# A decoder block on one core: state products behind the second own terms, second scores behind the first state products, key roots inverted by halves

## The chip, the core and the metric

One core of one Trainium2 chip runs the whole kernel. The metric is the device time in microseconds (us). PE is the matmul engine, PEld its weight loads, DVE, ACT and POOL the vector, scalar and general engines, SP the engine that issues most DMAs. Each engine runs its own list of instructions in program order; they meet only at semaphores.

## The reference

Three blocks follow each other on x of shape (16, 64, 256), each with a residual and a layernorm: a test-time-training recurrence, a cross attention over a context of 64 tokens, and a feed-forward block with int8-like rounding. The change touches the first block's loop and the scale of the attention keys. The recurrence goes over 4 chunks of 16 tokens, for each batch b and each of 16 heads of width 16:

```
kh      = k_i @ S                          # "state product" with the keys
g       = w * norm(kh) + b - (v_i - k_i);  v_new = norm-backward(g * w)
A       = tril(q_i @ k_i^T) * eta          # "scores"
qh      = q_i @ S - A @ v_new              # state product and "own term"
o       = q_i + (w * norm(qh) + b)
S       = S - (k_i * eta)^T @ v_new        # the own terms' other half
```

In the cross attention the scores are divided by the root mean square of each key over its 128 features (rmsnorm of k), head by head.

## The kernel before, in words

**Layout of the recurrence.** 16 batches and 16 heads are laid out as 32 groups g of 4 partition strips j. Each of the three products is 128 matmuls of 32x32 weights, for one half h (0 or 1) of the groups: `state_products(c, h)` (L508, recorded at L518), `own_terms(c, h)` (L522, recorded at L528) and `scores_ttt(c, h)` (L493, recorded at L500). Every matmul has a weight load of its own. State products read the state `st`, start the accumulation of `q S`, `k S` and S itself in PSUM; own terms add the new rows `ub` times the masked scores `ak`.

**The loop for chunk c and half h.** PE's `state_products(c, h)` ends; DVE's `state_read(c, h)` (L1425) copies kh, squares and sums it; ACT's `state_root` takes the root; DVE's `chain(c, h)` (L1432, 12 operations, then four `ub` writes, L1462) makes the update; PE's `own_terms(c, h)` adds it; DVE's `after_own_terms(c, h)` (L1511) copies qh and the new state, which releases `state_products(c + 1, h)`. DVE's own order within a chunk is: `state_read(c, 0)`; `kb_rows`, `a_masked`, `output_inverse(2c - 2)`, `out_c(c - 2)` (in chunk 1 the first two stand ahead of the read, the last two are absent); `chain(c, 0)`; `state_read(c, 1)`; `output_sums(2c - 1)`; `output_inverse(2c - 1)`, which waits for ACT's `output_root(2c - 1)` (L1080); `chain(c, 1)`; `out_normed`; `after_own_terms(c, 0)`; `out_gated(c - 1)`; `after_own_terms(c, 1)`; `output_sums(2c)`.

**The keys as filler.** Between these products PE makes the keys of the cross attention: 32 units (`key_unit`, PE L652, ACT L1065). A unit is one product into bank 6 or 7 (L659, two instructions), then on ACT a square (L1071) and a scaled copy (L1073). PE sums the squares of units four at a time (L650, eight instructions; units 0 to 3 right behind the matmul of unit 4, units 4 to 7 behind that of unit 8, and so on). A unit's square on ACT waits, from unit 4 on, for the sum of the unit four before it; a unit's matmul waits for the copy of the unit two before it. How many units stand at each place is in `KEY_PLACES`, read by the PE list and, with places merged, by the ACT list; ACT has its roots and squares of the recurrence between them.

**After the loop.** ACT takes the roots of all key sums (`krow`, L1076). PE runs `warm(4, 8)`, eight matmuls that nobody reads, waits for `k_rooted`, and begins a pipeline over 8 tiles of 128 tokens: `ttt_out` (L834), transposes (L842), `q_quarter` (L724), scores of the attention (L767), and so on. SP writes the key roots to DRAM and reads them back with other rows in two halves (`kroot`, `kinv`), DVE inverts both halves in one reciprocal (`key_scales`, L1549), and SP writes `kscale` and loads it, broadcast, as `rkb` for each tile. DVE's `scores_out(0)` (L1707) multiplies the first tile's scores by `rkb`; ACT's `exp_p(0)` depends on it and stands on ACT ahead of tile 1's second quarter. In that pipeline's step 0, DVE does `last_scale`, `last_gate`, `last_square`, `last_scale`, `last_out(2)`, which releases `ttt_out(2)` on PE, and then `key_scales`.

Of the kernel before, what the change touches and what calls it, by code (L numbers as in the profile page):

```python
# [36 lines left out]
B, T, D = 16, 64, 256  # L37
# [17 lines left out]
LT = NT - 1  # L55
KEY_PLACES = [(1, 2), (2, 2, 1, 1, 2, 1), (2, 2, 1, 1, 2, 1), (2, 3, 3, 3)]

def decoder_block(nc, x, ctx_in, Wq, Wk, Wv, Wo, Wbeta, ln_w, ln_b, Wg1, Wg2, norm_w,  # L60
                  XWq, XWk, XWv, XWo, gq, gk, w1_in, w2_in, out):
    stack = ExitStack()
    with stack:
# [315 lines left out]
        def _(sp):  # L379
# [36 lines left out]
            def roots_to_rows(half):  # L416
                sp.wait_ge(sem("k_rooted"), 1)
                for odd in range(2):
                    at = 64 * half + 32 * odd
                    sp.dma_start(kroot[half].rearrange("b (r o) t -> o r b t", o=2)[odd],  # L420
                                 krow[at:at + XH // 2, :].rearrange("p (b t) -> p b t", t=T)).then_inc(sem("k_rows_out"), 16)
                sp.wait_ge(sem("k_rows_out"), 32 * (half + 1))
                sp.dma_start(kinv[:, half * T:(half + 1) * T], kroot[half].rearrange("b h t -> (b h) t")).then_inc(sem("k_roots_in"), 16)

            def scales_out(half):
                sp.wait_ge(sem("k_inverted"), 1)
                sp.dma_start(kscale[half * B // 2:(half + 1) * B // 2, :].rearrange("b (h t) -> (b h) t", t=T),
                             kinv[:, half * T:(half + 1) * T]).then_inc(sem("k_scales_out"), 16)
# [43 lines left out]
        def _(pe):  # L472
# [204 lines left out]
            for c in range(1, NCH):  # L677
                places = iter(KEY_PLACES[c])
                state_products(c, 0)
                keys(next(places))  # L680
                state_products(c, 1)
                keys(next(places))
                if c < NCH - 1:
                    scores_ttt(c + 1, 0)
                    keys(next(places))
                own_terms(c, 0)
                if c < NCH - 1:
                    keys(next(places))
                    scores_ttt(c + 1, 1)
                keys(next(places))  # L690
                own_terms(c, 1)
                for n in places:
                    keys(n)
            key_unit(next(units))
# [149 lines left out]

            warm(4, 8)
            pe.wait_ge(sem("o_feat"), NCH)
# [104 lines left out]
        def _(act):  # L951
# [159 lines left out]
            for c in range(1, NCH):  # L1111
# [4 lines left out]
                output_square(c - 1)  # L1116
                keys(places[0])
                if c < NCH - 1:
                    k_blocks(c + 1)
                keys(places[1])  # L1120
                output_root(2 * c - 1)
                state_root(c, 1)
                for n in places[2:-2]:
                    keys(n)
                keys(places[-2])
                gated_square(c - 1)
                if c < NCH - 1:
                    keys(places[-1])
            last_root(0)
# [175 lines left out]
        def _(dve):  # L1305
# [240 lines left out]

            def key_scales():
                dve.wait_ge(sem("k_roots_in"), 32)
                V.reciprocal(kinv[:, :], kinv[:, :]).then_inc(sem("k_inverted"), 1)  # L1549

# [10 lines left out]
            for c in range(1, NCH):  # L1561
# [4 lines left out]
                if c >= 2:  # L1566
                    kb_rows(c)
                    a_masked(c)
                    output_inverse(2 * c - 2)
                    out_c(c - 2)  # L1570
                chain(c, 0)
                state_read(c, 1)
# [174 lines left out]
            for i, cur, prev, last2, last3, nxt, nxt2 in pipeline():  # L1747
                if i == 0:
                    last_scale(qhR, 2)
                    last_gate(2)  # L1750
                    last_square(sup, 3)
                    last_scale(sup, 3)
                    last_out(2)
                    key_scales()
                if nxt2:
# [195 lines left out]
```

## Time and profile before

| | |
|---|---|
| median of 3 runs | 381.57 us (378.9, 381.57, 383.26) |
| the profiled execution | 382.47 us, of which the span 380.7 us |
| PE, PEld busy | 344.8 us (91%), 242.8 us (64%) |
| DVE, ACT, POOL busy | 264.5 us (69%), 201.3 us (53%), 75.6 us (20%) |
| mean granted TensorE clock | 0.974 of full speed |
| chunks 1 to 3 of the recurrence | from about 70 to 146 us of the span |

The span counts from the first to the last instruction; the time has the launch around it. A clock of 1.0 is 2.4 GHz, 0.5 is 1.2 GHz. "Issue" in a row is idle time in which an engine waited for nothing that the profile shows. In a timeline, consecutive instructions of one line are merged, and a new row begins where there was a pause.

### The profile page before, as it was taken

To read this page: it belongs to the slowest core of one execution; us is meant where nothing else is said; L and a number is where in the kernel's file an instruction comes from. 1 tells how busy PE (TensorE), PEld (TensorE's weight loads), DVE (VectorE), ACT (ScalarE), POOL (GpSimd) and SP (SyncE) were. 2 spreads that over 40 slices of the span, in tenths; PEclk is the share of its full clock that TensorE was granted. 3 is DMA by queue.
4 is the path that set the end of the run, shared out by engine and by line. 5 is a ranking of instruction groups with operands and counts; after the bars stand their busy time and mean duration, and the time that the engine had idled before them with its cause. 6 is when DMAs were issued, how large, how long until landed. Compare 5 with 4: busy or idle time off the path is not lost.

```text
span 380.7 us, 11631 instructions
## 1 busy us (share of the span) xinstructions
PE 344.8 (91%) x5095; PEld 242.8 (64%) x5098; DVE 264.5 (69%) x536; ACT 201.3 (53%) x371; POOL 75.6 (20%) x91
## 2 busy tenths in 40 slices
PE   1999997998979877998999999999999999999974
PEld 1544585455435332587698796896977969866731
DVE  0499997897797899556263674855846739566795
ACT  1245974855525635255516556555555566576351
POOL 3009300000000000000062341522714505300100
PEclk9999999999987968999999999999999999999998
DMA  8997000000402001029120100200201000000000
GB/s 195 277 289 248 4 4 3 5 3 23 151 4 83 34 2 58 16 53 203 31 57 0 50 8 15 58 0 16 57 1 56 16 15 0 2 15 0 16 1 28
DMA packets 17986, 19.96 MB, mean 52 GB/s; under 512 B 3712, under 2 KB 15376, under 8 KB 17680
## 3 DMA queue, kind: packets, MB, share of 16 engines
q1 hardware_dynamic: 17328, 18.69, 18.8%
q8 instruction: 40, 0.66, 0.8%
q10 hardware_dynamic: 608, 0.54, 0.7%
q14 instruction: 10, 0.08, 0.1%
HBM read 18.04 MB, written 1.18 MB: 50 GB/s over the span
## 4 chain that ended last, share of the span: by engine, by line
PE 73%; DVE 15%; ACT 4%; issue 3%; DMA 3%; SPq 0%; POOLq 0%; POOL 0%; DVEq 0%
PE ps L790 14%; PE ps L724 12%; PE ps L547 6%; PE ps L659 5%; PE ps L782 5%; PE ps L767 4%; PE ps L500 3%; PE ps L809 2%; PE ps L528 2%; PE ps L740 2%; PE ps L518 2%; PE ps L617 2%; PE ps L650 2%; PE ps L758 2%; DMA xn<-in_x_dram 2%
## 5 line engine op out<-in xcount | busy, mean ns | idle before, releaser
L724 PEld LDWEIGHTS ps<-x1t,xwq 128*128 128x128 f32 x512 | 59.2, 192 | 6.4 <-issue 4.2
L724 PE MATMUL ps<-x1t,xwq 128*128 128x128 f32 x512 | 62.1, 278 | 0.7 <-ACT x1t L1188 0.7
L790 PE MATMUL ps<-mvo,cxp 128*128 128x256 f32 x224 | 51.8, 383 | 0.5 <-ACT cxp L1199 0.5
L1893 POOL TENSOR_SCALAR rstd<-mv 128x1 f32<-128x1 f32 x20 | 4.4, 218 | 212.6 <-DVE mv L1635 212.6
L790 PEld LDWEIGHTS ps<-mvo,cxp 128*128 128x128 f32 x224 | 41.3, 190 | 6.6 <-ACT cxp L1199 0.8
L659 PE MATMUL ps<-ctxt,xwk 128*128 128x512 f32 x64 | 39.1, 727 | 3.5 <-ACT kt L1073 2.3
L1151 ACT ACTIVATE qt<-ps 128x512 f32<-128x512 f32 x32 | 19.1, 596 | 33.9 <-PE ps L724 33.9
L1071 ACT ACTIVATE ksq<-ps 128x512 f32<-128x512 f32 x32 | 18.9, 591 | 21.4 <-PE ps L659 13.4
L1073 ACT ACTIVATE kt<-ps,gks 128x512 f32<-128x512 f32 x32 | 21.9, 683 | 0.0
L1158 ACT ACTIVATE qsq<-ps 128x512 f32<-128x512 f32 x32 | 19.0, 593 | 4.2 <-PE ps L740 4.2
L659 PEld LDWEIGHTS ps<-ctxt,xwk 128*128 128x128 f32 x64 | 11.9, 217 | 14.3 <-ACT kt L1073 6.2
L528 PEld LDWEIGHTS ps<-ak,ub 32*32 32x32 f32 x1024 | 11.9, 109 | 13.7 <-issue 13.5
L767 PEld LDWEIGHTS ps<-kt,qt 128*64 128x64 f32 x512 | 16.2, 138 | 6.8 <-ACT qt L1151 3.8
L528 PE MATMUL ps<-ak,ub 32*32 32x48 f32 (+1 forms) x1024 | 13.4, 200 | 6.9 <-DVE ub L1462 3.5
L1644 DVE TENSOR_SCALAR x<-rr,mv,rstd 128x256 f32<-128x256 f32 x16 | 6.6, 412 | 18.7 <-POOL rstd L1894 18.5
L782 PE MATMUL ps<-pt,ctx 64*128 64x512 f32 x64 | 18.5, 638 | 0.7 <-ACT pt L1178 0.7
L767 PE MATMUL ps<-kt,qt 128*64 128x64 f32 x512 | 18.4, 225 | 0.0
L1707 DVE TENSOR_TENSOR pr<-ps,rkb 128x1024 f32<-128x1024 f32 x8 | 9.8, 1224 | 12.2 <-PE ps L767 8.7
L1199 ACT ACTIVATE cxp<-ps 128x512 f32<-128x512 f32 x28 | 15.3, 606 | 4.5 <-PE ps L782 4.5
L1683 DVE TENSOR_TENSOR gs<-ps,s 128x352 f32<-128x352 f32 x16 | 8.3, 522 | 13.4 <-PE ps L809 13.2
L1908 POOL TENSOR_TENSOR rq<-rq,mhalf 128x16 f32<-128x16 f32 x6 | 17.4, 2908 | 0.5
L500 PEld LDWEIGHTS ps<-kqi,kb 32*32 32x32 f32 x1024 | 10.1, 110 | 7.8 <-issue 6.8
(238 smaller groups left out, 683.2 us busy)
## 6 DMA issues: line engine op xcount, KB each, us to landing
rkb<-kscale SPq DMA_DIRECT2D x16, 256.0 KB, 4.2
ctx<-in_ctx_dram SPq DMA_DIRECT2D x4, 512.0 KB, 8.7
xwo<-in_L_xattn_Wo_dram SPq DMA_DIRECT2D x1, 2048.0 KB, 14.2
xwq<-in_L_xattn_Wq_dram SPq DMA_DIRECT2D x4, 512.0 KB, 4.8
w1n<-in_L_ffn_w_gate_up_dram SPq DMA_DIRECT2D x1, 1408.0 KB, 9.9
xwv<-in_L_xattn_Wv_dram SPq DMA_DIRECT2D x1, 1024.0 KB, 11.2
xwk<-in_L_xattn_Wk_dram SPq DMA_DIRECT2D x1, 1024.0 KB, 16.5
xn<-in_x_dram SPq DMA_DIRECT2D x2, 512.0 KB, 5.9
```

The source lines that it names most:

```text
L500: last = mm(ps[part, 4 * BANK + g * C:4 * BANK + (g + 1) * C], kb[part, g * 32:(g + 1) * 32], kq[part, col:col + C], start=True, stop=True)
L528: last = mm(ps[part, g * GW + C:g * GW + C + w], ub[part, g * 32:(g + 1) * 32], ak[part, g * (C + 32):g * (C + 32) + w], start=c == 0 and ...
L547: last = mm(bank(bk), w[:, k * D + hh * P:k * D + (hh + 1) * P], xt[:, k * B * T + half * BANK:k * B * T + (half + 1) * BANK], start=k == ...
L659: mm(bank(6 + n % 2), xwk[:, h * XD:(h + 1) * XD], ctxt[:, half * BANK:(half + 1) * BANK], start=True, stop=True)\
L724: last = mm(bank(n % 2, P, t * P), xwq[qn][:, k * BANK + t * P:k * BANK + (t + 1) * P], x1t[:, (i % 2) * D + k * P:(i % 2) * D + (k + 1) * ...
L767: last = mm(ps[b2 * T:(b2 + 1) * T, 4 * BANK + h * T:4 * BANK + (h + 1) * T], qt[:, h * P + b2 * T:h * P + (b2 + 1) * T], kt[:, (i * XH + ...
L782: turn_done(mm(bank(bk), ctx2[rows, b * CD:(b + 1) * CD], pt[rows, :].rearrange("p (h q) -> p h q", q=P)[:, :, b2 * T:(b2 + 1) * T], start ...
L790: last = mm(bank(turn_banks[turn_of[("y", i, 0)]], D), context_of(i)[:, h * P:(h + 1) * P], mvo[:, h * D:(h + 1) * D], start=h == 0, stop= ...
L1071: A(ksq[n % 4][:, :], bank(6 + n % 2), ACT.Square).then_inc(sem("k_squared"), 1)
L1073: A(o, bank(6 + n % 2).rearrange("p (i t) -> p i t", t=P), ACT.Copy, scale=gks[:, 1:2]).then_inc(sem("key_emptied"), 1)
L1151: A(qt[:, qn * BANK:(qn + 1) * BANK], bank(n % 2), ACT.Copy).then_inc(sem("q_copied"), 1)
L1158: A(qsq[:, (n % 2) * BANK:(n % 2 + 1) * BANK], bank(n % 2), ACT.Square).then_inc(sem("q_squared"), 1)
```

## The change

It reorders three lists and cuts one instruction in two; except for five dummy matmuls nothing is added to or taken from the arithmetic.

- PE, loop: `scores_ttt(2, 1)` and `(3, 1)` move from between the own terms of the chunk before to behind the first state products of their own chunk. Behind `own_terms(c, 1)` no key units are left, so that the next chunk's state products follow directly.
- The key units' places are new. Per chunk, with s for state products, o for own terms, a for scores and numbers for units: before, chunk 1 was s0 2 s1 2 a(2,0) 1 o0 1 a(2,1) 2 o1 1, and so was chunk 2; chunk 3 was s0 2 s1 3 o0 3 o1 3. After, chunk 1 is s0 3 s1 2 a(2,0) 1 o0 3 o1; chunk 2 is s0 1 a(2,1) 1 s1 2 a(3,0) 1 o0 4 o1; chunk 3 is s0 1 a(3,1) 2 s1 2 o0 3 o1, and 3 units after it.
- ACT, loop: ahead of `output_root(2c - 1)` and `state_root(c, 1)` stood 2 + 2 units in chunks 1 and 2; now 3 + 3 stand there in chunk 1 and 2 + 3 in chunk 2.
- DVE, loop: `a_masked(c)` goes behind `output_inverse` and `out_c`.
- `warm(4, 8)` becomes `warm(4, 3)`.
- `key_scales` is done by halves: the first at the head of step 0, the second where it was. SP's `scales_out(half)` waits for its own half.

```diff
--- before.py
+++ after.py
@@ -53,7 +53,7 @@
 GW = 2 * C + 32
 NKU = 2 * XH
 LT = NT - 1
-KEY_PLACES = [(1, 2), (2, 2, 1, 1, 2, 1), (2, 2, 1, 1, 2, 1), (2, 3, 3, 3)]
+KEY_PLACES = [(1, 2), (1, 2, 2, 1, 3), (1, 1, 2, 1, 4), (1, 2, 2, 3, 3)]
 
 
 
@@ -420,10 +420,10 @@
                     sp.dma_start(kroot[half].rearrange("b (r o) t -> o r b t", o=2)[odd],
                                  krow[at:at + XH // 2, :].rearrange("p (b t) -> p b t", t=T)).then_inc(sem("k_rows_out"), 16)
                 sp.wait_ge(sem("k_rows_out"), 32 * (half + 1))
-                sp.dma_start(kinv[:, half * T:(half + 1) * T], kroot[half].rearrange("b h t -> (b h) t")).then_inc(sem("k_roots_in"), 16)
+                sp.dma_start(kinv[:, half * T:(half + 1) * T], kroot[half].rearrange("b h t -> (b h) t")).then_inc(sem("k_roots_in%d" % half), 16)
 
             def scales_out(half):
-                sp.wait_ge(sem("k_inverted"), 1)
+                sp.wait_ge(sem("k_inverted"), half + 1)
                 sp.dma_start(kscale[half * B // 2:(half + 1) * B // 2, :].rearrange("b (h t) -> (b h) t", t=T),
                              kinv[:, half * T:(half + 1) * T]).then_inc(sem("k_scales_out"), 16)
 
@@ -678,19 +678,18 @@
                 places = iter(KEY_PLACES[c])
                 state_products(c, 0)
                 keys(next(places))
+                if c >= 2:
+                    scores_ttt(c, 1)
+                keys(next(places))
                 state_products(c, 1)
                 keys(next(places))
                 if c < NCH - 1:
                     scores_ttt(c + 1, 0)
                     keys(next(places))
                 own_terms(c, 0)
-                if c < NCH - 1:
-                    keys(next(places))
-                    scores_ttt(c + 1, 1)
                 keys(next(places))
                 own_terms(c, 1)
-                for n in places:
-                    keys(n)
+            keys(next(places))
             key_unit(next(units))
 
 
@@ -842,7 +841,7 @@
                     last = nc.tensor.transpose(bank(bk, P, k * P), xn[:, i * D + k * P:i * D + (k + 1) * P], ident[:, :])
                 last.then_inc(sem("tp_done"), 1)
 
-            warm(4, 8)
+            warm(4, 3)
             pe.wait_ge(sem("o_feat"), NCH)
             pe.wait_ge(sem("wo_scaled"), KT)
             pe.wait_ge(sem("key_emptied"), NKU)
@@ -1114,18 +1113,16 @@
                 if c >= 2:
                     output_root(2 * c - 2)
                 output_square(c - 1)
-                keys(places[0])
+                keys(places[0] + places[1])
                 if c < NCH - 1:
                     k_blocks(c + 1)
-                keys(places[1])
+                    keys(places[2] + places[3])
+                else:
+                    keys(places[2])
                 output_root(2 * c - 1)
                 state_root(c, 1)
-                for n in places[2:-2]:
-                    keys(n)
-                keys(places[-2])
+                keys(places[4] if c < NCH - 1 else places[3])
                 gated_square(c - 1)
-                if c < NCH - 1:
-                    keys(places[-1])
             last_root(0)
             output_root(2 * NCH - 2)
             keys(1)
@@ -1544,9 +1541,10 @@
                 o = ogt[:, :].rearrange("p (a b c s) -> p c a b s", a=KT, b=B, c=NCH)[:, c]
                 V.transpose(o, oR[:, :]).then_inc(sem("o_feat"), 1)
 
-            def key_scales():
-                dve.wait_ge(sem("k_roots_in"), 32)
-                V.reciprocal(kinv[:, :], kinv[:, :]).then_inc(sem("k_inverted"), 1)
+            def key_scales(half):
+                own = kinv[:, half * T:(half + 1) * T]
+                dve.wait_ge(sem("k_roots_in%d" % half), 16)
+                V.reciprocal(own, own).then_inc(sem("k_inverted"), 1)
 
             kb_rows(0)
             weights_rounded("w2")
@@ -1565,9 +1563,9 @@
                 state_read(c, 0)
                 if c >= 2:
                     kb_rows(c)
-                    a_masked(c)
                     output_inverse(2 * c - 2)
                     out_c(c - 2)
+                    a_masked(c)
                 chain(c, 0)
                 state_read(c, 1)
                 output_sums(2 * c - 1)
@@ -1746,12 +1744,13 @@
             dve.wait_ge(sem("ld_x"), 32)
             for i, cur, prev, last2, last3, nxt, nxt2 in pipeline():
                 if i == 0:
+                    key_scales(0)
                     last_scale(qhR, 2)
                     last_gate(2)
                     last_square(sup, 3)
                     last_scale(sup, 3)
                     last_out(2)
-                    key_scales()
+                    key_scales(1)
                 if nxt2:
                     bk = turn("wo", i + 2)
                     freed(V.tensor_tensor(rw[:, :], bank(bk, D), xn[:, (i + 2) * D:(i + 3) * D], ALU.add), "wo", i + 2)
```

## Rows read from the trace of the kernel before

**Rows 1.** Waits between 66 and 156 us; columns: engine, line, releaser, total us, times, longest

```profile
DVE khR L1427 <- PE ps L518: 4.3, 2, 2.2
...
DVE qhR L1513 <- PE ps L528: 2.8, 2, 1.7
```

**Rows 2.** Timeline of PE, chunk 1 into 2; columns: start us, us, instructions, [idle before]

```profile
81.92 1.94 PE L528 MATMUL ps<-ak,ub 32*32 32x48 f32 x128
...
85.77 1.06 PE L650 MATMUL ps<-ksq,onehot 128*32 128x512 f32 x8 [0.84 <-issue]
86.76 1.19 PE L500 MATMUL ps<-kqi,kb 32*32 32x16 f32 x120
89.22 0.25 PE L500 MATMUL ps<-kqi,kb 32*32 32x16 f32 x8 [1.26 <-issue]
...
91.31 1.82 PE L528 MATMUL ps<-ak,ub 32*32 32x48 f32 x128
...
94.12 1.80 PE L518 MATMUL ps<-kqi,st 32*32 32x64 f32 x113
96.77 0.42 PE L518 MATMUL ps<-kqi,st 32*32 32x64 f32 x15 [0.85 <-issue]
```

**Rows 3.** Timeline of PE, chunks 2 and 3

```profile
105.97 0.44 PE L500 MATMUL ps<-kqi,kb 32*32 32x16 f32 x31 [0.63 <-issue]
...
111.34 0.71 PE L528 MATMUL ps<-ak,ub 32*32 32x48 f32 x42 [1.82 <-issue]
...
135.52 1.80 PE L528 MATMUL ps<-ak,ub 32*32 32x16 f32 x128 [3.04 <-DVE ub L1462]
```

**Rows 4.** Timeline of DVE, chunks 1 to 3

```profile
82.08 0.35 DVE L1525 RECIPROCAL ors<-osd 128x32 f32<-128x32 f32 x1 [0.39 <-ACT osd L1080]
...
87.96 0.48 DVE L1462 TENSOR_SCALAR ub<-us__111,mask_h 128x128 f32<-128x128 f32 x2
...
97.25 0.45 DVE L1427 STREAM_TRANSPOSE khR<-ps 128x256 f32<-128x256 f32 x1 [2.23 <-PE ps L518]
...
101.36 0.71 DVE L1545 STREAM_TRANSPOSE ogt<-oR 128x512 f32<-128x512 f32 x1
...
110.18 0.35 DVE L1525 RECIPROCAL ors<-osd 128x32 f32<-128x32 f32 x1 [0.39 <-ACT osd L1080]
...
124.70 0.45 DVE L1427 STREAM_TRANSPOSE khR<-ps 128x256 f32<-128x256 f32 x1 [2.10 <-PE ps L518]
```

**Rows 5.** Timeline of ACT, chunk 1

```profile
81.72 0.32 ACT L1080 ACTIVATE osd<-ovs,eps_t 128x32 f32<-128x32 f32 x1 [0.56 <-DVE ovs L1521]
...
86.91 0.60 ACT L1071 ACTIVATE ksq<-ps 128x512 f32<-128x512 f32 x1 [3.61 <-PE ps L650]
```

**Rows 6.** Windows; columns: stretch, length, busy PE, PEld, DVE, ACT, POOL, granted clock, DMA

```profile
135.00:138.00 3.00, 2.48 (x129) 2.22 (x130) 2.52 (x7) 0.52 (x2) 0.00 (x0) 0.62 0.03 5
```

**Rows 7.** Timeline of PE after the recurrence

```profile
153.75 1.67 PE L643 MATMUL ps<-w1t,ident_b 128*128 128x512 bf16 x7 [0.16 <-issue]
155.26 1.89 PE L834 MATMUL ps<-wo,ogt 128*128 128x256 f32 x8
...
180.49 0.43 PE L740 MATMUL ps<-qsq,onehot 128*32 128x128 f32 x8 [0.98 <-ACT qsq L1158]
```

**Rows 8.** Timeline of ACT, the key roots

```profile
153.62 0.69 ACT L1076 ACTIVATE krow<-ps,eps_t 128x512 f32<-128x512 f32 x1 [0.77 <-PE ps L650]
```

**Rows 9.** Timeline of SP's queue, the first reload of key roots

```profile
156.32 0.35 SPq L423 DMA_DIRECT2D kinv<-kroot  x1
```

**Rows 10.** View of DMAs; columns: transfer, queue, count, KB each, median us to landing

```profile
kinv<-kroot SPq DMA_DIRECT2D x2, 32.0 KB, 2.5
```

**Rows 11.** Timeline of DVE, key inversion and first scores

```profile
165.69 0.91 DVE L1549 RECIPROCAL kinv<-kinv 128x128 f32<-128x128 f32 x1
...
173.15 1.23 DVE L1707 TENSOR_TENSOR pr<-ps,rkb 128x1024 f32<-128x1024 f32 x1 [3.56 <-DMA rkb<-kscale]
```

**Rows 12.** Chain of waits, in order of time; columns: start us, us, what

```profile
168.69 4.34 DMA rkb<-kscale
```

## The prediction

> **What bounds the kernel now.** The shares of busy time come first: PE has 91% of the span, so it looks like the bound everywhere. Inside the recurrence that is not so simple, and the waits between 66 and 156 us say how: twice DVE waits for the state products (L518), 4.3 us in all, and twice for the second own terms (L528), 2.8 us [rows 1]. Those 7.1 us are the boundaries between chunks 1 and 2 and between 2 and 3. The timeline of PE shows what PE did meanwhile: the rows of chunk 1 have the last `ub` of half 1 written at 87.96 + 0.48 = 88.44 us [rows 4], but the own terms that use it start at 91.31 [rows 2], because scores (2, 1) and two key units stand ahead. Behind them one unit precedes the state products, which end at 97.19, and DVE reads them at 97.25 [rows 2, 4]. The change takes both obstacles away. Read by this alone it gives the whole 7.1 us.
>
> Two other things in the same rows speak against that, and the sum rests on them.
>
> First, PE stops inside runs of small matmuls, waiting for nothing the profile shows. The halts stand at fixed counts: between 85.77 and 89.22 lie 8 + 120 = 128 matmuls; from 89.22 to 96.77 lie 8 + 4 + 128 + 2 + 113 = 255 [rows 2]. So there is a crossing every 128 matmuls, each with its weight load, whatever their size. From one crossing to the next PE never got quicker than 89.22 - 85.77 = 3.45 us where it halted; the crossing ahead of 96.77 lies 116 matmuls into the own terms, at 91.31 + 116/128 x 1.75 = 92.9, so that one took 3.9, and in chunk 2 one halt took 1.82 us at 111.34 [rows 2, 3]. The next stretch of instructions seems to arrive no earlier. A product of 128 small matmuls lasts 1.3 to 2 us, so key units between products cost PE nothing: they fill time in which it would halt. The change puts own terms, state products, one unit and scores in a row.
>
> The Trainium skill, "Runtime: NRT & Kernel Launch", section "Instruction fetch mechanics", says that instructions come in 16 KiB blocks of 256 and that crossing a block is "mostly hidden". The trace agrees with the 256, which are 128 matmuls with their loads, and not with the rest. By that rule the sum would be that of the first rival below.
>
> Second, the order on ACT. DVE's `output_inverse(1)` stands ahead of `chain(1, 1)` and waits for ACT's `output_root(1)`: 0.39 us at 82.08 [rows 4]. The root now stands behind unit 8 on ACT, and unit 8's square waits for a PE sum.
>
> **Part by part, recurrence.** Chunk 1, the root. Up to the first own terms PE does the same set of work in another order, so unit 8 starts where they did, 81.92 [rows 2]. A unit takes 0.92 us (two between 89.47 and 91.31), a sum group 0.99 (85.77 to 86.76) [rows 2]. The group starts at 82.85, and ACT gets unit 8 a further 86.91 - 85.77 = 1.14 us on [rows 2, 5], at 84.0. Square and copy take about 1.1 (two operations like the one of 0.60 [rows 5]), so the root starts at 85.1 instead of 81.72 [rows 5]; if the crossing that now falls ahead of the group halts PE by 0.3, at 85.4. `chain(1, 1)` shifts by 3.4 to 3.7, I take 3.5: `ub` is done at 88.44 + 3.5 = 91.95, and the own terms start at 92.0, 0.7 later than before rather than 2.8 earlier.
>
> Chunk 1 into 2. DVE was free for `khR` at 97.25 - 2.23 = 95.02, and without its earlier wait of 1.7 it would be free 95.02 - 1.7 - 88.44 = 4.9 us behind `ub` [rows 1, 4]: now at 96.85. PE: the crossing falls 114 matmuls into the own terms (eight more were done ahead of them), at 93.6, the next 114 into state products, no earlier than 93.6 + 3.45 to 3.9 = 97.05 to 97.5, though PE alone would be there at 95.5. With 14 matmuls left they end at 97.3 to 97.8. DVE reads at about 97.6, against 97.25: 0.4 later. The gain of the boundary is gone.
>
> Chunk 2. `a_masked(2)` behind `out_c` costs nothing: before, `out_c` ended 101.36 + 0.71 - 97.25 = 4.8 us after the read with `a_masked` ahead of it, an operation of the same 512 columns, so DVE gets to it after some 4.1 us [rows 4]; scores (2, 1) end 3.7 after the state products even with the next crossing. If that cover goes, its whole lateness is on the path. The root again stands behind a fourth unit, 16. From the end of the first state products (97.6) PE does units 12 to 16, one sum group, scores (2, 1) and (3, 0) and products (2, 1): 5 x 0.92 + 0.99 + 2 x 1.27 + 2.04 = 10.2 us (scores 120 in 1.19, products 113 in 1.80 [rows 2]). That is 107.8; three crossings at 3.65 each from 97.4 make it 109.6. ACT's root follows 1.14 + 1.1 later, DVE 0.36 after that: 110.4 to 112.2, against 110.18 [rows 4]. I take 112.2, 2.0 later, since these crossings follow with little between them. `ub` then is done 6.36 us after it (as 88.44 - 82.08), at 118.5. Four units and sums behind the own terms end by about 117 at full clock and are covered.
>
> Chunk 2 into 3. DVE is free at 118.5 + 4.9 = 123.4. Own terms start at 118.6; crossings fall 72 matmuls into them, 119.6, and 72 into the state products, not ahead of 119.6 + 3.45 to 3.9 = 123.1 to 123.5; the rest takes 0.6. DVE reads at about 124.0 to 124.4 rather than 124.70 [rows 4]: I take 0.3 earlier. Chunk 3 has the same DVE work, its own terms waited 3.04 us for `ub` [rows 3], and ACT's unit total ahead of the root is unchanged: nothing more moves. Sum: -0.3 us.
>
> **The clock.** PE idle for 3.04 us ahead of 135.52 was followed by 1.2 GHz: the granted share of 135 to 138 is 0.62 [rows 3, 6]. Now PE idles about 3 us ahead of 92.0, then has only small matmuls. If the clock falls there, units and sums in chunk 2 take twice as long, ahead of a root that is on the path. Between nothing and 3.4 us (half of the five units and one group that can stand in it, and what they push); I take 1.0, nearer to nothing since DVE covers some.
>
> **After the loop.** Five dummies of 1.67 / 7 = 0.24 us less, but PE needs the key roots, done at 153.62 + 0.69 = 154.31; `ttt_out` started at 155.26 [rows 7, 8]. Gain 0.9. At most 1.2, at least 0 if the clock falls for want of them.
>
> The key halves. The first `kinv` was sent at 156.32 and lands 2.5 later, 158.8 [rows 9, 10], ahead of step 0 (about 160.6, less 0.9), so DVE doesn't wait. It spends on it between 0.35 (128x32, [rows 4]) and 0.91 (128x128 [rows 11]), say 0.5, ahead of `last_out(2)`: counted whole on PE. In return `rkb` comes early: its load of 4.34 us [rows 12] ended the 3.56 us that DVE waited for the first scores [rows 11]; what ends last then is the scores themselves, 0.9 earlier. That reaches PE through `exp_p(0)` and the 0.98 us wait at 180.49 [rows 7]. Net gain 0.9 - 0.5 = 0.4; bounds +0.5 and -0.9. If `rkb` were still late, the 0.5 would stay.
>
> **Sum.** -0.3 + 1.0 - 0.9 - 0.4 = -0.6 us. The profiled execution took 382.47, 0.9 above the median of 381.57; off the median this is **381.0 us**.
>
> **Rivals.**
> - *Halts do not follow the order* (0.27). The next stretch arrives while PE waits for `ub`, so that products follow directly. Then DVE is the bound: it reads at 96.85 (-0.4); the root of chunk 2 comes at 109.8, also -0.4; `ub` at 116.15, DVE free at 121.05 against 124.70: -3.65, with -0.9 and -0.4 about -5: 376.6. For it: other stretches pass without a halt. Against: halts stand in every product that follows another closely. The full 7.1 us would need the root on ACT to be early, which the list excludes.
> - *Longer halts and a low clock* (0.2), the slower side. From 105.97, where scores resumed, to 111.34 a stretch took 5.4 us [rows 3]. At 5.4 instead of 3.65 both boundaries lose 1.75 and chunk 2's root 1.5 more, +5; with the clock's full 3.4 in place of 1.0, +7.4 on -0.6: up to 388. It decides once stretches in chunk 2 take over 4.7 us, or `own_terms(2, 1)` waits for its four units; from there 385.5 to 388.
> - *The forecast* (0.53): the gain is eaten by ACT's root and by the halts.
>
> A measurement of this kernel can hardly tell 1% (3.8 us): its own three runs spread by 4.4. **Chances**: faster than 377.8 0.27, within 1% 0.53, slower 0.20. The forecast alone has 378.5 to 384.5; to leave out no more than 2 in 10 I go from **376.3 to 386.0**.
>
> **What would show it.** `ors` (L1525) of chunk 1 waits some 3.5 us for `osd`, behind `kt` of unit 8: the first step. `own_terms(1, 1)` at about 92.0 and a halt inside the state products right behind: the second; no halt there, and DVE without a wait for L518, would be the first rival. The granted clock between 92 and 105 tells the clock's term. `scores_out(0)` should end its wait on PE, not on `rkb`. If `ors` is not late, my reading of ACT's list is wrong, and the time is near 374.

## The result, and the profile after

The changed kernel takes 386.62 us (median of 4 runs, 385.84 to 387.25), the kernel before, beside it and with its first runs, 380.31 us (4 runs). The ratio is 1.0155, 95% interval 1.0082 to 1.0228: slower by 1.6%, or some 6 us. The forecast of 381.0 and the range up to 386.0 are missed; the time lies where the rival "longer halts and a low clock" had it (385.5 to 388), though it got there only in part by that rival's path. An execution that is over 1.5% slower than the fastest of its kernel is left out of every ratio below.

The span of the profiled execution is 384.1 us against 380.7. Its head, ahead of the recurrence, happened to be 1.3 us shorter, so I count from one event of the recurrence, DVE's first `khR` of chunk 1 (72.13 before, 70.84 after). First DVE in the kernel after, where each bracket is idle time and what ended it (L1424 is `state_read`, L1522 `output_inverse`, L1510 `after_own_terms`, L1411 `a_masked`):

```profile
70.84 0.43 DVE L1424 STREAM_TRANSPOSE khR<-ps 128x256 f32<-128x256 f32 x1
...
84.25 0.35 DVE L1522 RECIPROCAL ors<-osd 128x32 f32<-128x32 f32 x1 [3.85 <-ACT osd L1079]
...
94.79 0.45 DVE L1510 STREAM_TRANSPOSE qhR<-ps 128x256 f32<-128x256 f32 x1 [1.06 <-PE ps L528]
...
98.28 0.45 DVE L1424 STREAM_TRANSPOSE khR<-ps 128x256 f32<-128x256 f32 x1 [1.72 <-PE ps L518]
...
104.23 0.69 DVE L1411 TENSOR_TENSOR ak<-ps,tri 128x512 f32<-128x512 f32 x1 [1.73 <-PE ps L500]
...
114.76 0.35 DVE L1522 RECIPROCAL ors<-osd 128x32 f32<-128x32 f32 x1 [2.10 <-ACT osd L1079]
...
126.15 0.45 DVE L1424 STREAM_TRANSPOSE khR<-ps 128x256 f32<-128x256 f32 x1
...
132.96 0.69 DVE L1411 TENSOR_TENSOR ak<-ps,tri 128x512 f32<-128x512 f32 x1 [2.59 <-PE ps L500]
...
142.75 0.35 DVE L1522 RECIPROCAL ors<-osd 128x32 f32<-128x32 f32 x1 [1.36 <-ACT osd L1079]
```

Two of the waits at the same places in the kernel before (the others are in rows 1 and 4):

```profile
120.83 0.45 DVE L1513 STREAM_TRANSPOSE qhR<-ps 128x256 f32<-128x256 f32 x1 [1.16 <-PE ps L528]
...
137.63 0.35 DVE L1525 RECIPROCAL ors<-osd 128x32 f32<-128x32 f32 x1 [0.39 <-ACT osd L1080]
```

The loss can be read off as a sum, since DVE's own work hasn't changed. The two middle columns are the waits, and the running loss adds up what each wait after has more than the wait before.

| place | wait before | wait after | running loss |
|---|---|---|---|
| `ors`, chunk 1, for ACT's root [rows 4] | 0.39 | 3.85 | +3.5 |
| `qhR` and `khR`, chunk 1 into 2, for PE [rows 1] | 1.68 + 2.23 | 1.06 + 1.72 | +2.3 |
| `a_masked(2)`, for scores (2, 1) | 0 | 1.73 | +4.1 |
| `ors`, chunk 2 [rows 4] | 0.39 | 2.10 | +5.8 |
| `qhR` and `khR`, chunk 2 into 3 [rows 1] | 1.16 + 2.10 | 0 | +2.5 |
| `a_masked(3)`, for scores (3, 1) | 0 | 2.59 | +5.1 |
| `ors`, chunk 3 | 0.39 | 1.36 | +6.1 |

Counted by starts instead of waits, the last row is +6.4 (142.75 - 70.84 against 137.63 - 72.13). So the boundaries that the change is about were gained in part: 1.1 us from chunk 1 to 2, and from chunk 2 to 3 all 3.3 us. Five new or longer waits, 10.5 us in all, took more than twice that.

These are single executions. The changed loop repeats well: `khR` of chunk 3 comes 55.3 us behind that of chunk 1 here and in the experiment "Only the loop" below. The old loop does not: 52.6 us in the kernel before, 55.6 in the experiment "Only what stands behind the loop", whose loop is the same. There DVE waited longer for the state products:

```profile
127.10 0.45 DVE L1427 STREAM_TRANSPOSE khR<-ps 128x256 f32<-128x256 f32 x1 [3.57 <-PE ps L518]
```

The sum shows where this execution lost; how much the change costs is told by the ratios. On ACT the first of the five looks like this (L1070 is the square of unit 8, L1079 the root; the unit's copy stands between them):

```profile
82.83 0.60 ACT L1070 ACTIVATE ksq<-ps 128x512 f32<-128x512 f32 x1 [1.90 <-PE ps L650]
...
83.89 0.32 ACT L1079 ACTIVATE osd<-ovs,eps_t 128x32 f32<-128x32 f32 x1
```

The root stands behind unit 8, and its square waited 1.90 us for PE's sums. Now PE across the first boundary and in the two second scores (L528 own terms, L518 state products, L500 scores):

```profile
90.74 1.39 PE L528 MATMUL ps<-ak,ub 32*32 32x48 f32 x113 [1.78 <-DVE ub L1459]
94.12 0.46 PE L528 MATMUL ps<-ak,ub 32*32 32x48 f32 x12 [1.99 <-issue]
...
94.43 3.80 PE L518 MATMUL ps<-kqi,st 32*32 32x64 f32 x127
...
101.02 1.04 PE L500 MATMUL ps<-kqi,kb 32*32 32x16 f32 x103
103.78 0.38 PE L500 MATMUL ps<-kqi,kb 32*32 32x16 f32 x25 [1.72 <-issue]
...
125.40 0.70 PE L518 MATMUL ps<-kqi,st 32*32 32x32 f32 x58 [1.60 <-issue]
...
127.09 1.15 PE L500 MATMUL ps<-kqi,kb 32*32 32x16 f32 x68
131.87 1.04 PE L500 MATMUL ps<-kqi,kb 32*32 32x16 f32 x60 [3.64 <-issue]
```

The count of 128 holds: 12 + 1 + 3 + 127 matmuls, two of the unit, eight of sums and 103 of scores lie between the halt that ended at 94.12 and the one that ended at 103.78, 256 in all, one crossing having passed without a halt in the slow state products. From 125.40 to 131.87 it is 58 + 2 + 68 = 128. But that stretch lasted 6.5 us, where I had taken 3.65. SP's queue shows what ran beside both second scores, the loads of x and of the attention's Wq (two of the last three at once, the third behind the loop):

```profile
94.72 0.38 SPq L381 DMA_DIRECT2D xwq<-in_L_xattn_Wq_dram  x1
95.14 1.94 SPq L381 DMA_DIRECT2D xn<-in_x_dram  x2
124.27 26.65 SPq L381 DMA_DIRECT2D xwq<-in_L_xattn_Wq_dram  x3
```

They are sent when `own_terms(1, 1)` and `out_gated(1)` are done, which now is shortly ahead of the second scores. And the state products at 94.43 take 3.80 us, 30 ns a matmul instead of 16:

```profile
92.00:93.00 1.00, 0.14 (x15) 0.04 (x1) 1.00 (x2) 0.00 (x0) 0.00 (x0) 0.99 0.00 0
93.00:94.00 1.00, 0.00 (x0) 0.00 (x0) 0.70 (x2) 0.23 (x1) 0.00 (x0) 0.50 0.00 0
...
96.00:99.00 3.00, 3.00 (x80) 2.38 (x72) 1.24 (x3) 0.00 (x0) 0.00 (x0) 0.50 0.82 263
```

The granted clock (the number behind the five engines) is 0.50 there, 1.2 GHz. It fell at about 93.0, inside the halt that ended at 94.12; before that PE had stood idle for 1.78 us ahead of 90.74 and then done 1.39 us of small matmuls. It was low once more around the halt of 3.64 us (0.69 from 126 to 129, 0.50 from 129 to 135). Over the whole execution the clock is nearly what it was, 0.972 against 0.974, for the kernel before had its low stretches elsewhere (0.50 from 114 to 117).

### The profile page after: what moved, and what is told of

It reads as the page before. It is cut to its first block, busy times and chain, and to the rows that moved or that the text cites. A ratio compares the mean times of both kernels' runs of the same rounds, so it can differ in the third digit from the quotient of the medians.

```text
span 384.1 us, 11625 instructions
## 1 busy us (share of the span) xinstructions
PE 343.0 (89%) x5093; PEld 242.1 (63%) x5093; DVE 264.6 (69%) x537; ACT 201.5 (52%) x371; POOL 75.7 (20%) x91
## 4 chain that ended last, share of the span: by engine, by line
PE 73%; DVE 14%; ACT 6%; issue 4%; DMA 1%; SPq 0%; POOLq 0%; POOL 0%; DVEq 0%
PE ps L789 14%; PE ps L723 13%; PE ps L547 5%; PE ps L766 5%; PE ps L781 4%; PE ps L659 4%; PE ps L500 3%; PE ps L518 3%; PE ps L808 2%; PE ps L739 2%; PE ps L650 2%; PE ps L617 2%; PE ps L833 2%; PE ps L757 2%; DMA xn<-in_x_dram 1%
## 5 line engine op out<-in xcount | busy, mean ns | idle before, releaser
L659 PE MATMUL ps<-ctxt,xwk 128*128 128x512 f32 x64 | 37.4, 694 | 3.4 <-ACT kt L1072 2.2
L1070 ACT ACTIVATE ksq<-ps 128x512 f32<-128x512 f32 x32 | 19.0, 594 | 24.9 <-PE ps L659 15.6
L528 PEld LDWEIGHTS ps<-ak,ub 32*32 32x32 f32 x1024 | 11.4, 105 | 15.7 <-issue 15.7
L528 PE MATMUL ps<-ak,ub 32*32 32x48 f32 (+1 forms) x1024 | 12.9, 197 | 9.1 <-issue 4.6
L500 PEld LDWEIGHTS ps<-kqi,kb 32*32 32x32 f32 x1024 | 10.2, 110 | 10.7 <-issue 9.7
```

The lines of the kernel that those rows point to most:

```text
L500: last = mm(ps[part, 4 * BANK + g * C:4 * BANK + (g + 1) * C], kb[part, g * 32:(g + 1) * 32], kq[part, col:col + C], start=True, stop=True)
L528: last = mm(ps[part, g * GW + C:g * GW + C + w], ub[part, g * 32:(g + 1) * 32], ak[part, g * (C + 32):g * (C + 32) + w], start=c == 0 and ...
L659: mm(bank(6 + n % 2), xwk[:, h * XD:(h + 1) * XD], ctxt[:, half * BANK:(half + 1) * BANK], start=True, stop=True)\
L1070: A(ksq[n % 4][:, :], bank(6 + n % 2), ACT.Square).then_inc(sem("k_squared"), 1)
```

## Experiments

All ratios are against the kernel before, measured beside them, with 95% intervals. 1% is 3.8 us.

**Only what stands behind the loop.**

```diff
 # on the kernel before
-            warm(4, 8)
+            warm(4, 3)
 ...
+                    key_scales(0)            # ahead of last_scale(qhR, 2)
 ...
-                    key_scales()
+                    key_scales(1)
```

> The kernel before with the two edits behind the loop alone: three dummy matmuls instead of eight, key roots inverted by halves. Theory 'loop' (all of the loss comes from the reordered recurrence): same as before or slightly faster, 0 to -1.3 us, most likely -0.6, since between krow and ttt_out some 0.7 us go and the halves give nothing. Rival 'tail' (the lost dummies or the earlier reciprocal cost something later): slower than before by over 1 us.

Measured: 381.54 us, ratio 0.9966 (0.9923 to 1.0009). The tail does not cost; a gain isn't shown.

**Only the loop.** The reverse edit, on the changed kernel.

> The changed kernel with its two edits behind the loop undone, so that only the reordered recurrence is left. Theory 'loop': slower than before by 5.5 to 7 us. Rival 'tail': within 3 us of before.

Measured: 389.87 us, 1.0199 (1.0109 to 1.0290), some 7.6 us slower, a little more than expected. The whole loss is the reordered recurrence; the rival "tail" falls.

**Roots ahead of the units on ACT.**

```diff
 # on the changed kernel
-                    keys(places[2] + places[3])
-                else:
-                    keys(places[2])
+                    keys(places[2])
                 output_root(2 * c - 1)
                 state_root(c, 1)
-                keys(places[4] if c < NCH - 1 else places[3])
+                keys(places[3] + places[4] if c < NCH - 1 else places[2] + places[3])
```

> The changed kernel, but on ACT output_root(2c-1) and state_root(c, 1) stand ahead of units 8, 16 and 24 instead of behind them. Theory 'roots' (the waits of 3.85, 2.10 and 1.36 us of L1522 for osd are on the path): they shrink to some 0.4 and the kernel gains 3 to 6 us on the changed one, ending near the kernel before. Rival 'halts and clock' (PE is so late through its halts and the low clock that the root's lateness is covered): gain under 1.5 us.

Measured: 381.78 us, 0.9986 (0.9942 to 1.0029), 1.7% better than the changed kernel. DVE in this kernel (L1520 `output_inverse`, L1409 `a_masked`):

```profile
81.29 0.35 DVE L1520 RECIPROCAL ors<-osd 128x32 f32<-128x32 f32 x1 [0.79 <-ACT osd L1079]
...
101.28 0.69 DVE L1409 TENSOR_TENSOR ak<-ps,tri 128x512 f32<-128x512 f32 x1 [1.68 <-PE ps L500]
...
128.01 0.65 DVE L1409 TENSOR_TENSOR ak<-ps,tri 128x512 f32<-128x512 f32 x1
```

The waits for the root are 0.79, 0.39 and 0.39 us where they were 3.85, 2.10 and 1.36. PE kept its full clock up to 123 us. `a_masked(2)` still waits 1.68. The theory "roots" holds; the gain, some 6.4 us, is even a little above the 3 to 6 that were expected. But it is not the price of the waits for the root alone. With the roots early `out_gated(1)` is early too, the second set of loads starts at 119.63, and the halt in scores (3, 1) is 0.37 us instead of 3.64: `a_masked(3)`, at 128.01, waits for nothing. So this run also cures the low clock and a part of what the loads did.

**Loads behind the loop.**

```diff
 # on the changed kernel
-            sp.wait_ge(sem("mg_done"), 2 * 2)
-            load_xwq(0)
-            load_x()
             sp.wait_ge(sem("og_ready"), 2)
-            load_xwq(1)
-            load_xwq(2)
             sp.wait_ge(sem("mg_done"), 2 * NCH)
+            load_x()
+            load_xwq(0)
+            load_xwq(1)
+            load_xwq(2)
             load_xwq(3)
```

> The changed kernel with the loads of x and of Wq of the attention (3 MB) all sent behind the last own terms instead of within chunks 2 and 3. Theory 'loads' (they hold up the instructions of PE: halts of 1.72 and 3.64 us in the second scores come while they run or just after): these halts fall below 1 us, the waits of L1411 (1.73 and 2.59 us) with them, and the kernel gains 2 to 5 us, less what the pipeline waits for its first data. Rival 'fixed' (a stretch of 128 matmuls takes its time whatever the loads do): halts as before, no gain or a loss of up to 2 us.

Measured: 382.19 us, 1.0028 (0.9987 to 1.0069), 1.3% better than the changed kernel with no compute instruction moved. The second scores of chunk 3 on PE, then DVE (L1410 `a_masked`):

```profile
128.41 0.69 PE L499 MATMUL ps<-kqi,kb 32*32 32x16 f32 x60 [1.01 <-issue]
```

```profile
103.62 0.65 DVE L1410 TENSOR_TENSOR ak<-ps,tri 128x512 f32<-128x512 f32 x1
...
129.85 0.65 DVE L1410 TENSOR_TENSOR ak<-ps,tri 128x512 f32<-128x512 f32 x1
```

The halt in scores (3, 1) is 1.01 instead of 3.64 us, in scores (2, 1) there is none, and `a_masked` waits for neither. "Fixed" falls: a stretch of instructions takes longer while the loads run. The price comes behind the loop, where DVE waits 1.72 us for the first `kinv`, whose DMA now meets the loads.

**Both, with the loads one step earlier.** The roots as above, and the loads of x and three parts of Wq sent after `own_terms(3, 0)`, where PE has key units and one last product.

```diff
 # on the kernel with the roots ahead
-            sp.wait_ge(sem("mg_done"), 2 * 2)
-            load_xwq(0)
-            load_x()
             sp.wait_ge(sem("og_ready"), 2)
+            sp.wait_ge(sem("mg_done"), 2 * NCH - 1)
+            load_xwq(0)
+            load_x()
             load_xwq(1)
```

> The changed kernel with the roots ahead of units 8, 16 and 24 on ACT, and with x and the first three parts of Wq loaded only once own_terms(3, 0) are done, so that no load runs beside the second scores. Theory 'two causes' (late roots and loads that hold up PE's instructions add up): some 3 us better than the roots alone, 376 to 380 us, and faster than the kernel before by 3 to 6 us; no wait of L1411, none of L1522 above 0.4. Rival 'one cause' (whichever is cured, the other's time comes back as a halt or a wait): no better than the roots alone, 380 to 383.

Measured: 378.5 us, 0.9923 (0.9898 to 0.9948), about 2.9 us faster than the kernel before. That is 0.6% better than the roots alone, with intervals that just overlap, and 2.3% better than the changed kernel, where roots and loads by themselves gave 1.7% and 1.3%. So curing both is better than curing one, but the two overlap and do not add up in full. The expected wait of at most 0.4 us for the root was missed in chunk 1, where it is 0.79. PE's halts and DVE's waits that remain:

```profile
93.01 0.33 PE L528 MATMUL ps<-ak,ub 32*32 32x48 f32 x12 [1.29 <-issue]
...
96.74 0.42 PE L518 MATMUL ps<-kqi,st 32*32 32x64 f32 x15 [1.80 <-issue]
...
122.30 0.70 PE L518 MATMUL ps<-kqi,st 32*32 32x32 f32 x58 [2.04 <-issue]
...
126.30 0.69 PE L500 MATMUL ps<-kqi,kb 32*32 32x16 f32 x60 [1.55 <-issue]
```

```profile
93.51 0.45 DVE L1508 STREAM_TRANSPOSE qhR<-ps 128x256 f32<-128x256 f32 x1 [2.26 <-PE ps L528]
...
97.22 0.45 DVE L1422 STREAM_TRANSPOSE khR<-ps 128x256 f32<-128x256 f32 x1 [1.94 <-PE ps L518]
...
123.04 0.45 DVE L1422 STREAM_TRANSPOSE khR<-ps 128x256 f32<-128x256 f32 x1 [1.51 <-PE ps L518]
```

No load runs here, the clock is full up to 126, and the halts are still there: 93.01 to 96.74 and 122.30 to 126.30 are stretches of 3.7 and 4.0 us. This is the floor that the prediction meant. DVE waits 2.26 + 1.94 us for it at the first boundary, about what it waited before the change (3.9), and 1.51 at the second, where it had waited 3.3. Neither `a_masked` waits. The pauses of 1.29 and 1.80 us at the place where the changed kernel lost its clock left it at 1.00 here.

**Dummy matmuls against the falling clock.**

```diff
 # on the changed kernel, between own_terms(c, 0) and own_terms(c, 1)
                 keys(next(places))
+                if c == 1:
+                    pe.wait_ge(sem("key_emptied"), 11)
+                    warm(6, 7)
                 own_terms(c, 1)
```

> The changed kernel with seven dummy matmuls (1.6 us) in PE's idle time ahead of own_terms(1, 1). Theory 'clock' (the idle ahead of it lets the clock fall, and the 127 state products at half clock, 3.80 us instead of 2, make khR of chunk 2 late): the clock stays at 2.4 GHz through 93 to 100, but a halt of about 1.5 us returns inside these state products, as the stretch of instructions is then the limit; gain 0 to 2 us. Rival 'clock is all': khR of chunk 2 comes 1.9 us earlier, the kernel gains 2 to 3 us.

Measured: 386.8 us, 1.0116 (1.0047 to 1.0184). The interval overlaps with that of the changed kernel, so the time alone decides nothing; the trace shows the place itself:

```profile
93.00:96.00 3.00, 2.06 (x136) 1.76 (x125) 2.90 (x6) 0.63 (x1) 0.00 (x0) 1.00 0.52 142
```

```profile
91.70 1.56 PE L528 MATMUL ps<-ak,ub 32*32 32x48 f32 x128 [0.42 <-DVE ub L1462]
...
95.95 0.53 PE L518 MATMUL ps<-kqi,st 32*32 32x64 f32 x22 [0.77 <-issue]
...
102.15 0.44 PE L500 MATMUL ps<-kqi,kb 32*32 32x16 f32 x32 [2.69 <-issue]
```

```profile
96.53 0.45 DVE L1427 STREAM_TRANSPOSE khR<-ps 128x256 f32<-128x256 f32 x1
```

The clock stays at 1.00 up to 102 and `khR` of chunk 2 comes 24.7 us behind that of chunk 1 (71.79 in this trace) instead of 27.4. That is 2.7 us, more than even the rival had said. Only some 1.7 of them are the clock: without halts and waits, own terms and state products took 5.5 us in the changed kernel (90.74 to 98.23) and take 3.8 here (91.70 to 96.48). The rest is a halt: the own terms, which stopped for 1.99 us in the changed kernel, run through, and 0.77 comes back in the state products. So the dummies changed two things, and this run isn't a test of the clock alone. In the scores, where the loads run, PE halts for 2.69 us and `a_masked` waits 1.90. The run's gain of 0.4%, about 1.5 us, lies with "clock" (0 to 2); it isn't clear of zero, and too near to the rival's 2 to 3 to tell them apart.

**Half of the scores.** In scores (2, 1) and (3, 1), strips 2 and 3 aren't computed, so this kernel leaves out part of the recurrence; it is there only to be timed.

```diff
+                    if c >= 2 and h == 1 and j >= 2:
+                        continue
```

> The changed kernel with half of scores (2, 1) and (3, 1) left out (strips 2 and 3 aren't computed): 64 matmuls fewer in each. Theory 'stretches': what costs is the count of instructions; each is 0.6 us less of matmul time, yet the waits of L1411 for these scores (1.73 and 2.59 us) fall by more than 1.2 each, to under 0.5 and under 1.4, since the crossing moves behind them; gain 2 to 5 us. Rival 'matmul time': each wait falls by 0.6, gain 1 to 1.5 us.

Measured: 384.13 us, 1.0089 (1.0052 to 1.0126), 0.7% or 2.5 us better than the changed kernel, with overlapping intervals. DVE (L1413 `a_masked`) and PE (L502 scores):

```profile
104.18 0.65 DVE L1413 TENSOR_TENSOR ak<-ps,tri 128x512 f32<-128x512 f32 x1
...
132.19 0.69 DVE L1413 TENSOR_TENSOR ak<-ps,tri 128x512 f32<-128x512 f32 x1 [1.76 <-PE ps L502]
```

```profile
128.11 0.29 PE L502 MATMUL ps<-kqi,kb 32*32 32x16 f32 x4
130.36 1.78 PE L502 MATMUL ps<-kqi,kb 32*32 32x16 f32 x60 [1.96 <-issue]
```

The wait for scores (2, 1) went from 1.73 to nothing, far more than the 0.6 us of matmul time: PE's halt comes behind them, 0.67 us in the state products that follow. That for (3, 1) went from 2.59 to 1.76, by 0.8 only, since there a crossing still falls inside, after 4 matmuls, while the loads run (and the 60 behind it run at half clock). One expectation is confirmed, one missed; both fit that what counts is whether a crossing lies in the way.

**The loads alone, on the kernel before.** The same edit of SP's list as in "Both, with the loads one step earlier".

> The kernel before with x and the first three parts of Wq loaded only once own_terms(3, 0) are done. Theory 'loads matter where small matmuls follow closely': here units stand between, PE has slack, and only the halts of 0.85 and 0.47 us ahead of khR shrink: between no change and 1.5 us faster. Rival 'loads always cost': 3 us or more faster, as the changed kernel gained 4.4 by it.

Measured: 379.5 us, 0.9936 (0.9904 to 0.9969), some 2.4 us faster: between the two expectations. The loads cost the kernel before too, about half of the 1.3% that they cost the changed one, and as much as the 0.6% that they cost the changed one with its roots ahead.

**Both orders at their best.** Each gets the late loads, `warm(4, 3)`, and key roots by halves with the first half moved:

```diff
 # on the changed kernel's order behind the loop
                 if i == 0:
-                    key_scales(0)
                     last_scale(qhR, 2)
                     last_gate(2)
                     last_square(sup, 3)
+                    key_scales(0)
                     last_scale(sup, 3)
```

The old order of the recurrence:

> The kernel before with the loads moved behind own_terms(3, 0), three dummies instead of eight, and key roots inverted by halves, the first half where DVE would wait for ACT's root anyway (ahead of the second last_scale of step 0). Theory 'sum': the loads gave 2.4 us, the tail 1.3, together 0.9900 of before, 378 us; the first half in this place delays ttt_out(2) by 0.1 instead of 0.35 us. Rival 'the same time twice' (both recover the same slack): 0.9935, as with the loads alone.

Measured: 380.58 us, 0.9961 (0.9927 to 0.9996). From `ttt_out` to the end of the wait for `qsq` it has 24.9 us, the changed kernel 25.3: the 0.35 us are saved, but the sum of 0.9900 isn't reached, and the interval holds the rival's 0.9935.

The new order, with its roots ahead:

> The changed kernel with roots ahead of units 8, 16 and 24, loads behind own_terms(3, 0), and the first key inversion ahead of the second last_scale. Theory 'order adds nothing' (both orders of the recurrence are held by the same stretches of instructions, so what is left of the reordering is worth under 1 us): within 0.3% of the kernel before with the same loads and tail. Rival 'the reordering is good once its roots and loads are right': 0.5% or more faster than that one.

Measured: 379.24 us, 0.9917 (0.9887 to 0.9948), 0.44% below the other, with overlapping intervals. From `khR` of chunk 1 to that of chunk 3 the new order needs 51.7 us, the old one 52.6. The theory (within 0.3%) and the rival (0.5% or more) are both left standing. The reordering itself is worth 0.9 us by these two traces and 1.7 by the medians' ratios, and isn't clear of nothing. This version, the one of 378.5 us and the two with the old order have intervals below 1.

## Why the prediction was wrong

Delays against the kernel before, as the prediction had them and as they came (the running loss from above):

| place | forecast | measured |
|---|---|---|
| `ors`, chunk 1 | +3.5 | +3.5 |
| `khR`, chunk 2 | +0.4 | +2.3 |
| `a_masked(2)` | covered | +4.1 |
| `ors`, chunk 2 | +2.0 | +5.8 |
| `khR`, chunk 3 | -0.3 | +2.5 |
| `a_masked(3)` | nothing moves | +5.1 |
| `ors`, chunk 3 | -0.3, with the clock's 1.0 +0.7 | +6.1 |

**The first step was right in mechanism and size.** The root behind unit 8 was to shift `chain(1, 1)` by 3.5 us; it shifted by 3.46, and the own terms start at 90.74, which with the shorter head of 1.29 is the 92.0 of the prediction. Putting the roots ahead gave 1.7% together with what hung on it. That the direct succession of own terms and state products gives little while PE halts every 128 matmuls was right too: with roots and loads cured, 5.7 of the old 7.2 us of waits are still there [rows 1].

**The step that failed is the size of the crossings.** "Three crossings at 3.65 each", and the same 3.45 to 3.9 at each boundary, took the shortest stretches of the trace before. Three things came of it.

*The halt in the own terms.* The prediction let the first crossing, 114 matmuls into `own_terms(1, 1)`, pass without a halt: its 3.45 to 3.9 us, reckoned from the crossing before, were long over. There PE halted for 1.99 us, until 3.4 us after it had begun again at 90.74. The views of DMA transfers show why: the page counts PE's instructions as 5093 matmuls and 5093 weight loads, 39.8 times 256, and it has a queue with 40 transfers.

```profile
q8 instruction: 40, 0.66, 0.7%
```

That is 40 blocks of 16 KB. None of them runs from 85.2 to 91.7 us, all of PE's idle time included; the one that PE needs runs from 91.81 to 92.78, that is 1.1 us after PE began again:

```profile
DMA packets 0, 0.00 MB, mean 0 GB/s; under 512 B 0, under 2 KB 0, under 8 KB 0
```

```profile
q8 instruction: 1, 0.02, 5.0%
```

The first is the stretch from 85.2 to 91.7, the second that from 91.7 to 92.9. With this the condition of the first rival, that the next stretch arrives while PE waits for `ub`, did not come about here. With the dummies the block came early, from 87.03 to 87.97, and the halt was gone. This halt and the low clock behind it are what made `khR` of chunk 2 later than forecast, by 1.9 us.

*The loads.* The change moves two sets of loads, released by `own_terms(1, 1)` and `out_gated(1)`, to shortly ahead of runs of small matmuls, and stretches are longer beside them: 6.5 us in scores (3, 1), and a halt of 1.72 in scores (2, 1). I had gone through SP's queue only for the key roots. The halt of 3.64 us ended at 131.87. In the 4.05 us behind the crossing ahead of it (125.4 to 129.4) the loads' packets run and no block of instructions; it starts at 129.45, with the last packet of the loads. Without loads, in the experiment "Loads behind the loop", it starts 1.1 us behind the same crossing, at 126.06. In order, the changed kernel from 125.4 to 129.4 and from 129.4 to 130.5, and that run from 126.0 to 127.2:

```profile
q1 hardware_dynamic: 536, 1.03, 81.0%
```

```profile
q8 instruction: 1, 0.02, 5.7%
```

```profile
q8 instruction: 1, 0.02, 5.3%
```

In all twelve traces, each of the 81 halts between 70 and 150 us ends 1.2 to 1.6 us behind the end of such a transfer. So PE does wait for its instructions, and the loads do put that transfer off: in the four traces with loads beside scores (3, 1) it starts 3.4 to 4.1 us behind the crossing ahead of them, in three without loads 1.1 to 1.6. With the roots ahead and the loads begun earlier it is 1.9 us.

Moving the loads, with nothing else, gave 1.3%, about 5 us. Not all of it is part of the miss, for the kernel before gains 0.6% by nearly the same edit and the forecast was reckoned from that kernel. By the ratios 2.4 us are the change's own, by the two waits of `a_masked` 4.3; the runs don't settle between them.

*Long stretches without loads.* The 5.4 us from 105.97 to 111.34 in the kernel before [rows 3], which the prediction set aside for its rival, have no load beside them: from 105.9 to 109.1 no packet of any queue runs, and the block starts only at 109.15. What held it up there is open.

**"`a_masked(2)` behind `out_c` costs nothing"** fell with the crossings. Named cover: scores (2, 1) end 3.7 us after the state products, DVE gets there after 4.1. Measured: the scores ended 104.16 - 98.23 = 5.9 us after, and DVE waited 1.73. **"Nothing more moves" in chunk 3** missed the same wait, 2.59 us, and the root behind it, 1.0. In the same part, three crossings at 3.65 from 97.4 make 108.35 and not 109.6; no term names the 1.25 us between.

**The clock** was the term with the widest bounds, 0 to 3.4, taken at 1.0. It fell where I said, but it made the state products themselves slow, some 1.7 us at `khR` of chunk 2, where I had counted only units and sums. How much of the 1.7% of the roots is the wait, how much the clock and how much the loads that came to lie elsewhere, the runs don't separate.

**Behind the loop.** `ttt_out` follows the end of `krow` by 0.25 us instead of 0.95: 0.7 gained, 0.9 said. The halves were to give 0.4; here is what they did, on DVE, PE and ACT:

```profile
176.49 1.23 DVE L1705 TENSOR_TENSOR pr<-ps,rkb 128x1024 f32<-128x1024 f32 x1 [2.76 <-PE ps L766]
```

```profile
169.96 1.13 PE L833 MATMUL ps<-wo,ogt 128*128 128x256 f32 x4 [0.35 <-DVE ogt L1605]
...
184.24 0.43 PE L739 MATMUL ps<-qsq,onehot 128*32 128x128 f32 x8 [0.59 <-ACT qsq L1155]
```

```profile
182.16 1.06 ACT L1205 ACTIVATE pr<-pr 128x1024 f32<-128x1024 f32 x1
```

The first inversion takes 0.55 us, as said. DVE waits for the scores on PE, no longer for `rkb` [rows 11], and the wait for `qsq` fell from 0.98 to 0.59 [rows 7], since `exp_p(0)` on ACT no longer waits for DVE (0.40 us before). But `ttt_out(2)` waits 0.35 for the delayed `last_out(2)`: net nothing, 25.33 us from `ttt_out` to the end of that wait against 25.23.

**The chances.** The rival whose range holds the time had 0.20. Its halts and its clock came true: the block ahead of scores (2, 1) starts 6.0 us behind the one before it, and the clock was low. Its path did not: neither did the boundary from chunk 2 to 3 lose, nor did `own_terms(2, 1)` wait for its units. The time went to the two waits of `a_masked`, which that rival doesn't have, so that its figure fits is in part luck. The forecast took the middle of terms that can come together: in the changed kernel halts, late scores and a low clock all did. They need not, for with the roots ahead the halts and one late score were there at full clock.

The Trainium skill, "Runtime: NRT & Kernel Launch", section "Instruction fetch mechanics", calls the crossing of a block of 256 instructions mostly hidden, and says that the sequencer fetches blocks by a DMA queue of its own. The count and the queue agree with all kernels here; "mostly hidden" does not hold for products of 32x32 matmuls, with halts of up to 3.7 us.

## What to carry to other kernels

Before moving work on one engine, list what the moved completion releases elsewhere, the DMA queue first: the same loads cost more where they came to lie beside a run of tiny instructions. Where an engine halts at a fixed count of instructions, filler between the small products fills time in which it would halt, and taking it out gained little here (0.4%, not clear of noise). When a stretch has been seen at 3.45 and at 5.4 us, a sum of several belongs between both, and not at the short end. And a short operation that another engine waits for (here a root of 0.3 us) must not stand behind filler whose own input comes late.

## What the runs showed of the hardware

- PE halts for instructions at every 128th matmul (each has a weight load) unless the next block is there. Each halt ends 1.2 to 1.6 us behind the end of a 16 KB transfer of an instruction queue (81 halts in twelve traces). Where it halts twice in a row, at full clock and without other loads, the shortest stretches are 3.45 to 4.0 us, and one took 5.4.
- Data loads put that transfer off. Beside 1 MB of loads a stretch took 6.5 us and the block started 4.05 us behind the crossing; without them it started 1.1 us behind it.
- At a granted clock of 0.50 the 32x32 matmuls slow down as well: 30 ns instead of 16 for 64 columns.
- A pause of 1.8 us, 1.4 us of small matmuls and 0.9 us of a second pause were followed by 1.2 GHz; with 1.7 us of dummy matmuls in the first pause it stayed at 2.4 GHz, and so it did in another run with pauses of 1.3 and 1.8 us.
